# A conv and gated feed-forward kernel on one core: opening order of the first group, and the conv bias as a column

## The chip, the core and the metric

The kernel runs on one core of a Trainium2 chip. The metric is the device time of one launch in microseconds (us). A core has TensorE (PE in the profile; its weight loads are PEld), VectorE (DVE), ScalarE (ACT), GpSimd (POOL) and SyncE (SP), which here only issues DMAs. Each runs its own instructions in order and waits for the others through semaphores.

## What is computed

```python
# x 128x32x512, cond_128 128x128, fside_S_0 32
out = lax.conv_general_dilated(x, weight, window_strides=(1,), padding=[(4, 4)],
                               dimension_numbers=('NCH', 'OIH', 'NCH'), feature_group_count=4)
ctx = jnp.einsum('nd,od->no', c, c_weight)
out = out + ctx[:, :, None] + bias[None, :, None]
...
up = xt @ W_up.T            # xt: 4096 rows of 512; F = 1376
gate = jax.nn.silu(xt @ W_gate.T)
y = gate * up @ W_down.T
x = x + y
```

## The kernel before, in words

The 32 channels form four groups (`G`) of eight. For each group the conv output (1024 rows of 512) is the moving operand of the gate and up products, whose 1376 rows are taken in eleven chunks `f` of 128; then come the down products. Every fp32 product is made of three products of "hi" and "lo" parts (`terms`), so each weight and each operand is first split: ScalarE writes the hi part (line 843, `split_h`, `w_raw`, `w_mixed`), VectorE the lo part (line 1070).

From chunk 1 on, a chunk's gate and up blocks for both halves of the rows come from seven products (kinds 0 to 6) instead of eight, in the manner of Strassen and Winograd. These need sums of operands (`K_S1`, `K_S2`, `K_S3`, `K_S4`, made from the staged conv output by `mix_h_first`) and sums of weights (T1 and T2 by VectorE, lines 1134 and 1138; T3 and T4 by GpSimd, `mix_t`, lines 513 and 514, which then also makes their lo parts, line 521). `prepare(f, part)` is ScalarE's and VectorE's share of chunk f's weights: part 0 keeps the turned gate block, part 1 the up block and T1, T2; part 2 splits T1 and T2, part 3 splits T3 and T4. `RAW_A1`, `RAW_A2`, `RAW_B1`, `RAW_B2` are plain parts of the conv output; `q` counts their two K blocks. Chunk 0 of group 0 uses eight plain products (`first_half`, `second_half`, line 725), so that it can start before any sum exists.

Before that, TensorE turns the conv weights, the context weights (`turn_ctx`) and x, runs eight conv steps (lines 624 and 629), and makes `ctxb`, the context product plus bias, 128 rows per group, with two fp32 products per group: one with `cond_t` (line 576), one of a single contraction row, the repeated bias against a row of ones (line 577). VectorE adds `ctxb` as it reads each conv step out of PSUM (`read_conv`), SP re-lays each read step by DMA into `stage` (32 window DMAs, `stage_window`, line 336, two of them from ScalarE's queue), and behind these SP issues the loads of chunk 2's gate and up weights into `w_nat` (`load_nat(2)`) and of the next group's x (`load_x(1, 0)`). `wrap` is a copy of four columns that GpSimd makes for each loaded weight block; TensorE turns the block only after it. `block_x` is GpSimd's reordering of x for the next group's conv.

Every engine's order is written out by hand. Waits that matter below, in the kernel's words: `product(0, 1, 5)` (kind 5 of chunk 1, line 711) waits for `copied4`, which is ScalarE's `copy_chain(1, 1, 4)`, since it overwrites the bank that is copied; `product(0, 1, 1)` waits for `silu_a_done`, VectorE's first step of `first_gated(0)`, which follows ScalarE's `first_sigmoids`; `product(0, 1, 2)` waits for `w_made[K_S2]`, the lo part of T2; second_half's products wait per q for VectorE's lo part of `RAW_A2` and `RAW_B2`, whose source is the staged conv output.

## Time and profile before

| | us |
|---|---|
| median of three runs (764.04 to 764.9) | 764.38 |
| the profiled execution's own time | 765.41 |
| its span, first to last instruction | 763.6 |
| TensorE busy in the span | 749.9 |

The span is measured by the hardware profiler in one execution. What lies around it, 765.41 - 763.6 = 1.8 us, is launch and end. A timeline row reads: start and duration in us, engine, line, operation, output<-inputs, shapes and how many instructions are merged; in brackets how long the engine stood idle before it and what released it. Times are from the span's start.

### The profile page before, as it was taken

The page shows a single profiled execution, that of the slowest core. Times are in us where ns is not written, and L with a number is a line of the kernel's source. Part 1 is how long each engine was busy: PE and PEld are TensorE (multiplying, and loading weights), DVE is VectorE, ACT ScalarE, POOL GpSimd, SP SyncE. Part 2 cuts the span into 40 slices and gives each one's busy share as a digit, 9 for nine tenths or more (in the row PEclk, how much of TensorE's full clock was granted, in tenths as well). Part 3 has the DMA queues.
Part 4 walks back from the last instruction along what each step waited for, and adds up shares of the span by engine and source line. Part 5 has one row for each costly group of instructions (what it writes and reads, how often), then busy time and mean ns, then how long its engine had stood idle before and what let it go on. Part 6 is the DMA issues. An engine that isn't in the chain of part 4 may idle for free.

```text
span 763.6 us, 10287 instructions
## 1 busy us (share of the span) xinstructions
PE 749.9 (98%) x3465; PEld 611.4 (80%) x3465; DVE 426.9 (56%) x703; ACT 275.3 (36%) x519; POOL 79.6 (10%) x111
## 2 busy tenths in 40 slices
PE   7989999999999999999999999999999999999998
PEld 6768888878888887887888878787788888887886
DVE  3897776764765555446735545445763444445224
ACT  4555555443433233324422332233431233333221
POOL 4334434110000111001000100100000000000000
PEclk9999999999999999999999999999999999999999
DMA  6486666679988578667435867667443876766412
GB/s 184 125 316 235 222 226 236 219 221 312 356 266 262 166 206 221 172 179 218 163 114 187 268 176 209 193 191 218 140 140 109 295 197 195 193 191 181 140 27 111
DMA packets 113684, 152.37 MB, mean 200 GB/s; under 512 B 11138, under 2 KB 49186, under 8 KB 113634
## 3 DMA queue, kind: packets, MB, share of 16 engines
q1 hardware_dynamic: 113152, 151.51, 63.7%
q8 instruction: 29, 0.48, 0.3%
q10 hardware_dynamic: 482, 0.21, 0.1%
q14 instruction: 21, 0.17, 0.1%
HBM read 108.95 MB, written 34.34 MB: 188 GB/s over the span
## 4 chain that ended last, share of the span: by engine, by line
PE 90%; issue 3%; SPq 2%; DMA 2%; DVE 1%; POOL 1%; ACT 0%; POOLq 0%; DVEq 0%
PE bank L711 51%; PE bank L774 31%; PE bank L624 2%; PE bank L629 2%; PE bank L604 2%; SPq L336 2%; DMA stage<-win 1%; PE bank L667 1%; PE bank L638 1%; PE bank L649 0%; DVE g_all L1277 0%; POOL g_all L526 0%; PE bank L586 0%; DVE win L1162 0%; POOL t_all L513 0%
## 5 line engine op out<-in xcount | busy, mean ns | idle before, releaser
L711 PE MATMUL bank<-hc_hi,ring 128*128 128x512 f32 (+1 forms) x1204 | 376.5, 394 | 5.0 <-DVE ring L1070 2.0
L711 PEld LDWEIGHTS bank<-hc_hi,ring 128*128 128x128 f32 (+1 forms) x1204 | 219.5, 185 | 54.6 <-issue 5.0
L711 PE MATMUL bank<-hc_lo,ring 128*128 128x512 f32 (+1 forms) x602 | 235.1, 391 | 0.0
L774 PE MATMUL bank<-ring,g_hi 128*128 128x512 f32 (+1 forms) x704 | 218.6, 392 | 0.0
L774 PEld LDWEIGHTS bank<-ring,g_hi 128*128 128x128 f32 (+1 forms) x704 | 131.2, 188 | 28.0 <-DVE g_lo L1070 0.8
L843 ACT ACTIVATE mix<-bank 128x512 f32<-128x512 f32 (+1 forms) x129 | 77.1, 598 | 208.5 <-PE bank L711 208.5
L774 PE MATMUL bank<-ring,g_lo 128*128 128x512 f32 (+1 forms) x352 | 137.1, 390 | 0.0
L711 PEld LDWEIGHTS bank<-hc_lo,ring 128*128 128x128 f32 (+1 forms) x602 | 111.5, 185 | 26.2
L1070 DVE TENSOR_TENSOR g_lo<-g_all,g_hi 128x512 fp32r<-128x512 f32 (+1 forms) x88 | 60.9, 695 | 83.7 <-ACT g_hi L843 83.7
L843 ACT ACTIVATE g_hi<-g_all 128x512 fp32r<-128x512 f32 (+1 forms) x88 | 55.1, 629 | 114.1 <-PE bank L774 114.0
L1243 DVE TENSOR_TENSOR mix<-bank,mix 128x512 f32<-128x512 f32 (+1 forms) x43 | 29.7, 691 | 87.2 <-ACT mix L960 87.0
L774 PEld LDWEIGHTS bank<-ring,g_lo 128*128 128x128 f32 (+1 forms) x352 | 66.1, 188 | 14.1
L305 POOL COPY x_blk<-x_in 128x512 f32<-128x512 f32 x24 | 28.0, 1166 | 325.5 <-DMA x_in<-in_x 166.4
L1238 DVE TENSOR_TENSOR mix<-bank,mix 128x512 f32<-128x512 f32 (+1 forms) x43 | 29.5, 687 | 37.5 <-ACT mix L843 37.5
L1233 DVE TENSOR_TENSOR mix<-mix 128x512 f32<-128x512 f32 (+1 forms) x43 | 29.7, 692 | 34.8 <-ACT mix L954 34.7
L960 ACT ACTIVATE mix<-bank 128x512 f32<-128x512 f32 (+1 forms) x43 | 25.7, 598 | 43.2 <-PE bank L711 43.2
L1228 DVE TENSOR_TENSOR mix<-bank,mix 128x512 f32<-128x512 f32 (+1 forms) x43 | 29.7, 691 | 11.2 <-PE bank L711 6.0
L843 ACT ACTIVATE xt_hi<-bank 128x512 fp32r<-128x512 f32 (+1 forms) x33 | 15.9, 510 | 55.1 <-PE bank L604 55.1
L1248 DVE TENSOR_TENSOR mix<-bank,mix 128x512 f32<-128x512 f32 (+1 forms) x43 | 29.7, 691 | 8.1 <-PE bank L711 6.8
L1162 DVE TENSOR_TENSOR win<-bank,ctxb 128x512 f32<-128x512 f32 (+1 forms) x24 | 16.1, 670 | 30.4 <-DMA stage<-win 21.5
L1070 DVE TENSOR_TENSOR hc_lo<-stage,hc_hi 128x512 fp32r<-128x512 f32 x50 | 32.6, 691 | 0.8 <-ACT hc_hi L843 0.7
L843 ACT ACTIVATE hc_hi<-stage 128x512 fp32r<-128x512 f32 x50 | 28.6, 618 | 2.9 <-DMA stage<-g_all 2.8
(141 smaller groups left out, 562.1 us busy)
## 6 DMA issues: line engine op xcount, KB each, us to landing
ring<-saved SPq DMA_DIRECT2D x319, 256.0 KB, 2.9
saved<-ring SPq DMA_DIRECT2D x99, 256.0 KB, 2.6
g_all<-in_x SPq DMA_DIRECT2D x32, 256.0 KB, 3.7
out_y<-g_all SPq DMA_DIRECT2D x32, 256.0 KB, 3.6
x_in<-in_x SPq DMA_DIRECT2D x13, 512.0 KB, 5.1
stage<-win SPq DMA_DIRECT2D x96, 64.0 KB, 2.8
w_nat<-in_L_ffn_W_gate SPq DMA_DIRECT2D x10, 256.0 KB, 3.9
w_nat<-in_L_ffn_W_up SPq DMA_DIRECT2D x10, 256.0 KB, 3.9
```

The lines of the kernel that those rows point to most:

```text
L305: copy(blocks(grp, k)[:, :, :, :], x_place(grp, k // 2)[:, :, r0:r0 + WB * R] .rearrange("n c (b r) -> n b r c", r=R)).then_inc(x_blocked_ ...
L711: mm = pe.matmul(bank[0:w, :], wt, hv, start=fresh and q == 0 and t == 0, stop=q == 1 and t == 2, skip_group_check=not fresh)
L774: mm = pe.matmul(acc(half, tt)[:], gs, wd, start=f == 0 and t == 0, stop=f == FC - 1 and t == 2)
L843: return act.activation(dst, src, ACT.Copy)
L960: act.activation(act_b[0:w], chain_ps[f % 2][0:w, :], ACT.Sigmoid).then_inc(sig_b_done, 1)
L1070: return dve.tensor_tensor(dst, src, hi_part.bitcast(F32), ALU.subtract)
L1162: last = dve.tensor_tensor(to[:, w0:w0 + n, :], conv_bank(grp, k)[:, 0:n * P].rearrange("p (w n) -> p w n", w=n), ctxb[:, grp:grp + 1, :]. ...
L1228: dve.tensor_tensor(act_a[0:w], second_ps[0:w, :], copy0[0:w], ALU.add).then_inc(gate_a_done, 1)
L1233: dve.tensor_tensor(act_a[0:w], act_a[0:w], sig_a[0:w], ALU.mult).then_inc(silu_a_done, 1)
L1238: dve.tensor_tensor(copy4[0:w], third_ps[0:w, :], copy4[0:w], ALU.add).then_inc(up_b_done, 1)
L1243: dve.tensor_tensor(act_b[0:w], chain_ps[f % 2][0:w, :], act_b[0:w], ALU.mult).then_inc(silu_b_done, 1)
L1248: dve.tensor_tensor(copy2[0:w], third_ps[0:w, :], copy2[0:w], ALU.add).then_inc(up_a_done, 1)
```

## The change

Nothing is computed differently except the bias. Its parts:

1. The bias no longer enters by 1x128 products against a row of ones. `turn_ctx` makes four fp32 products of one output column each (the repeated bias of a group against one element of `ones`) into four spare columns of `gate_ps`; ScalarE copies these to `bias_col`, and `keep_ctx` now makes one activation per group with the column as its bias.
2. TensorE turns the up block of chunk 1 before `first_half` instead of behind it, and the context products of groups 1 to 3 stand between the q halves of `first_half`'s first product. The wait for the last conv read moves behind that product.
3. ScalarE and VectorE do all of chunk 1's `prepare` parts ahead of, or between, the splits of `RAW_A2` and `RAW_B2`; `K_S3`'s splits move behind those of `K_S1` and `K_S2`. GpSimd wraps chunk 2's weights first and does `mix_t(1)`, `mix_t_lo(1)` before `block_x(1, 0)`.
4. In chunk 1, `K_S4`'s splits move behind `prepare(2, 1)` and `prepare(2, 2)` on both engines; on ScalarE they now stand directly ahead of `copy_chain(1, 1, 4)`.

```diff
@@ gpsimd
             mix_h_first(1)
+            wrap(2)
             for g in range(G):
                 for f in range(FC):
-                    if g + 1 < G and f == 0:
-                        block_x(g + 1, 0)
-                    if g == 0 and f + 2 < FC:
+                    if g == 0 and 0 < f < FC - 2:
                         wrap(f + 2)
                     if g == 0 and f + 1 < FC:
                         mix_t(f + 1)
                         mix_t_lo(f + 1)
+                    if g + 1 < G and f == 0:
+                        block_x(g + 1, 0)
@@ tensor
-                pe.transpose(gate_ps[:, 0:P], cond_nat, ident[:]).then_inc(ctx_mm, 1)
+                pe.transpose(gate_ps[:, 0:P], cond_nat, ident[:])
+                pe.wait_ge(consts, 8)
+                for g in range(G):
+                    mm = pe.matmul(gate_ps[:, P + g:P + g + 1], bias_rep[:, g, :], ones[:, 0:1], start=True, stop=True, skip_group_check=True)
+                mm.then_inc(ctx_mm, 1)
...
                 for g in groups:
-                    to = ctx_bank(g)[:, g * P:(g + 1) * P]
-                    pe.matmul(to, ctx_w_rep[:, g, :, :], cond_t, start=True, stop=False)
-                    mm = pe.matmul(to, bias_rep[:, g, :], ones, start=False, stop=True)
+                    mm = pe.matmul(ctx_bank(g)[:, g * P:(g + 1) * P], ctx_w_rep[:, g, :, :], cond_t, start=True, stop=True)
...
             def first_half():
                 pe.wait_ge(t_lo_done, 1)
+                pe.wait_ge(w_made[RAW_A1], 1)
+                plain(RAW_A1, RAW_A1, second_ps, True, parts=(0,))
+                ctx_products(range(1, G))
+                plain(RAW_A1, RAW_A1, second_ps, True, parts=(1,))
                 pe.wait_ge(conv_out, CPG)
-                pe.wait_ge(w_made[RAW_A1], 1)
-                plain(RAW_A1, RAW_A1, second_ps, True)
...
             turn_gate(1)
-            ctx_products(range(1, G))
+            turn_up(1)
             first_half()
-            turn_up(1)
             second_half()
@@ scalar
             def keep_ctx(n, groups):
                 act.wait_ge(ctx_mm, n + 1)
-                hi(ctxb[:, groups, :], ctx_bank(n - 1)[:].rearrange("p (g n) -> p g n", g=G)[:, groups, :]).then_inc(ctx_done, 1)
+                for g in groups:
+                    last = act.activation(ctxb[:, g, :], ctx_bank(g)[:, g * P:(g + 1) * P], ACT.Identity, bias=bias_col[:, g:g + 1])
+                last.then_inc(ctx_done, 1)
...
             prepare(1, 0)
-            keep_ctx(2, slice(1, G))
-            split_h(0, K_S3, 0)
-            split_h(0, K_S3, 1)
-            for q in range(2):
-                split_h(0, RAW_A2, q)
-                split_h(0, RAW_B2, q)
             prepare(1, 1)
-            for kind in (K_S1, K_S2):
+            keep_ctx(2, range(1, G))
+            split_h(0, RAW_A2, 0)
+            split_h(0, RAW_B2, 0)
+            prepare(1, 2)
+            split_h(0, RAW_A2, 1)
+            split_h(0, RAW_B2, 1)
+            prepare(1, 3)
+            for kind in (K_S1, K_S2, K_S3):
                 split_h(0, kind, 0)
                 split_h(0, kind, 1)
             first_sigmoids()
-            prepare(1, 2)
-            prepare(1, 3)
...
                     sigmoid_a(n, f)
-                    if n == 1:
-                        split_h(0, K_S4, 0)
-                        split_h(0, K_S4, 1)
...
                         prepare(f + 1, 2)
+                    if n == 1:
+                        split_h(0, K_S4, 0)
+                        split_h(0, K_S4, 1)
                     copy_chain(n, f, 4)
@@ vector
             prepare(1, 0)
-            split_h(0, K_S3, 0)
-            split_h(0, K_S3, 1)
-            for q in range(2):
-                split_h(0, RAW_A2, q)
-                split_h(0, RAW_B2, q)
+            prepare(1, 1)
+            split_h(0, RAW_A2, 0)
+            split_h(0, RAW_B2, 0)
+            prepare(1, 2)
+            split_h(0, RAW_A2, 1)
+            split_h(0, RAW_B2, 1)
             for kind in (K_S1, K_S2):
                 mix_h_first(kind, 0)
                 mix_h_first(kind, 1)
-            prepare(1, 1)
+            split_h(0, K_S2, 0)
+            split_h(0, K_S2, 1)
             first_gated(0)
-            for kind in (K_S2, K_S1):
-                split_h(0, kind, 0)
-                split_h(0, kind, 1)
+            split_h(0, K_S1, 0)
+            split_h(0, K_S1, 1)
+            split_h(0, K_S3, 0)
+            split_h(0, K_S3, 1)
             first_gated(1)
-            prepare(1, 2)
...
-                    if n == 1:
-                        split_h(0, K_S4, 0)
-                        split_h(0, K_S4, 1)
...
                         prepare(f + 1, 2)
+                    if n == 1:
+                        split_h(0, K_S4, 0)
+                        split_h(0, K_S4, 1)
```

On VectorE, from the splits of the staged conv output (`hc_lo<-stage`) to the first gated result (`g_all<-bank,mix`), before; `g_all<-stage` and `g_all<-g_all,stage` are the sums of operands, `ring<-bank` and the two `t_all` rows are chunk 1's up block, T1 and T2:

```order
L1070 TENSOR_TENSOR ring<-x_gate,ring 128x256 x2
L1070 TENSOR_TENSOR hc_lo<-g_all,hc_hi 128x512 x2
L1070 TENSOR_TENSOR hc_lo<-stage,hc_hi 128x512 x4
L1177 TENSOR_TENSOR g_all<-stage 128x512 x2
L1181 TENSOR_TENSOR g_all<-g_all,stage 128x512 x2
L1070 TENSOR_TENSOR ring<-bank,ring 128x256
L1134 TENSOR_TENSOR t_all<-bank,x_gate 128x256
L1138 TENSOR_TENSOR t_all<-bank,t_all 128x256
L1218 TENSOR_TENSOR mix<-bank,mix 128x512
L1221 TENSOR_TENSOR g_all<-bank,mix 128x512
```

and in the changed program:

```order
L1075 TENSOR_TENSOR ring<-x_gate,ring 128x256 x2
L1075 TENSOR_TENSOR ring<-bank,ring 128x256
L1139 TENSOR_TENSOR t_all<-bank,x_gate 128x256
L1143 TENSOR_TENSOR t_all<-bank,t_all 128x256
L1075 TENSOR_TENSOR hc_lo<-stage,hc_hi 128x512 x2
L1075 TENSOR_TENSOR ring<-t_all,ring 128x256 x2
L1075 TENSOR_TENSOR hc_lo<-stage,hc_hi 128x512 x2
L1182 TENSOR_TENSOR g_all<-stage 128x512 x2
L1186 TENSOR_TENSOR g_all<-g_all,stage 128x512 x2
L1075 TENSOR_TENSOR hc_lo<-g_all,hc_hi 128x512 x2
L1223 TENSOR_TENSOR mix<-bank,mix 128x512
```

T1, T2 and their lo parts went ahead of the sums; the split of K_S3 left its place ahead of the staged parts and one pair of operand splits (K_S2) now stands ahead of the gated result.

On ScalarE, chunk 1 from the copy of its second chain bank (the first row) to the copy of its fourth (`mix<-bank`, the last but one row), before; `mix<-mix` is a sigmoid, `hc_hi<-g_all` the split of K_S4, `ring<-bank` and `ring<-t_all` are chunk 2's up block and T1, T2:

```order
L843 ACTIVATE mix<-bank 128x512
L954 ACTIVATE mix<-mix 128x512
L843 ACTIVATE hc_hi<-g_all 128x512 x2
L843 ACTIVATE ring<-bank 128x256
L843 ACTIVATE ring<-t_all 128x256 x2
L843 ACTIVATE mix<-bank 128x512
L843 ACTIVATE ring<-t_all 128x256 x2
```

and in the changed program:

```order
L847 ACTIVATE mix<-bank 128x512
L958 ACTIVATE mix<-mix 128x512
L847 ACTIVATE ring<-bank 128x256
L847 ACTIVATE ring<-t_all 128x256 x2
L847 ACTIVATE hc_hi<-g_all 128x512 x2
L847 ACTIVATE mix<-bank 128x512
L847 ACTIVATE ring<-t_all 128x256 x2
```

The two splits of K_S4 now stand between T1, T2 and the copy.

On ScalarE a little earlier, from the first splits of the staged A2, B2 parts to the sigmoids (L937, L939), in the changed program; before, the four `ring<-t_all` rows of chunk 1 all stood behind the two sigmoids, and K_S3's two splits ahead of the staged parts:

```order
L847 ACTIVATE hc_hi<-stage 128x512 x2
L847 ACTIVATE ring<-t_all 128x256 x2
L847 ACTIVATE hc_hi<-stage 128x512 x2
L847 ACTIVATE ring<-t_all 128x256 x2
L847 ACTIVATE hc_hi<-g_all 128x512 x6
L937 ACTIVATE mix<-bank 128x512
```

The second `ring<-t_all x2` splits T3 and T4, which GpSimd makes, and six operand splits and the sigmoids are queued behind it.

## Rows read from the trace of the kernel before

**Rows 1.** The page: busy time of each engine, share, instructions.

```profile
PE 749.9 (98%) x3465; PEld 611.4 (80%) x3465; DVE 426.9 (56%) x703; ACT 275.3 (36%) x519; POOL 79.6 (10%) x111
```

**Rows 2.** Waits of TensorE after 90 us: total, times, longest.

```profile
PE bank L711 <- DVE mix L1238: 1.9, 3, 0.8
```

**Rows 3.** Timeline of TensorE, 29 to 58 us.

```profile
29.38 0.39 PE L576 MATMUL bank<-g_all 128*128 128x128 f32 x2
...
31.78 0.72 PE L725 MATMUL bank<-hc_hi,ring 128*128 128x512 f32 x2
...
45.07 0.66 PE L638 MATMUL bank<-ident,w_nat 128*128 128x128 f32 x4 [0.27 <-POOL w_nat L505]
...
49.95 0.73 PE L711 MATMUL bank<-hc_hi,ring 128*128 128x512 f32 x2 [1.97 <-DVE ring L1070]
...
55.75 0.40 PE L711 MATMUL bank<-hc_lo,ring 128*128 128x512 f32 x1
57.35 0.70 PE L711 MATMUL bank<-hc_hi,ring 128*128 128x512 f32 x2 [1.20 <-issue]
```

**Rows 4.** Timeline of ScalarE, 36 to 58 us.

```profile
36.98 1.15 ACT L843 ACTIVATE hc_hi<-stage 128x512 fp32r<-128x512 f32 x2 [1.04 <-DMA stage<-g_all]
...
41.92 0.58 ACT L933 ACTIVATE mix<-bank 128x512 f32<-128x512 f32 x1
...
52.65 1.14 ACT L843 ACTIVATE hc_hi<-g_all 128x512 fp32r<-128x512 f32 x2
...
55.89 0.87 ACT L843 ACTIVATE ring<-t_all 128x256 fp32r<-128x256 f32 x2 [1.82 <-DVE t_all L1134]
56.67 0.58 ACT L843 ACTIVATE mix<-bank 128x512 f32<-128x512 f32 x1
```

**Rows 5.** Timeline of VectorE, 38 to 56 us.

```profile
38.86 1.29 DVE L1177 TENSOR_TENSOR g_all<-stage 128x512 f32<-128x512 f32 x2
...
42.54 0.69 DVE L1218 TENSOR_TENSOR mix<-bank,mix 128x512 f32<-128x512 f32 x1
...
43.87 3.44 DVE L1070 TENSOR_TENSOR hc_lo<-g_all,hc_hi 128x512 fp32r<-128x512 f32 x4
47.24 0.68 DVE L1218 TENSOR_TENSOR mix<-bank,mix 128x512 f32<-128x512 f32 x1
...
49.81 0.68 DVE L1228 TENSOR_TENSOR mix<-bank,mix 128x512 f32<-128x512 f32 x1
...
55.36 0.41 DVE L1134 TENSOR_TENSOR t_all<-bank,x_gate 128x256 f32<-128x256 f32 x1
```

**Rows 6.** The chain that ended last, 6 to 16 us: start, us, what.

```profile
6.78 1.93 PE bank L604 x8
...
9.52 0.72 PE bank L577 x2
...
13.23 1.28 PE bank L629 x3
...
15.20 0.70 PE bank L624 x3
```

**Rows 7.** Timeline of TensorE's weight loads, 9.4 to 10.1 us.

```profile
9.45 0.50 PEld L577 LDWEIGHTS bank<-g_all 1*128 1x128 f32 x2 [0.23 <-issue]
```

**Rows 8.** Timeline of SP's queue, 15 to 36 us.

```profile
15.27 19.66 SPq L336 DMA_DIRECT2D stage<-g_all  x30
34.97 0.59 SPq L352 DMA_DIRECT2D w_nat<-in_L_ffn_W_gate  x1
```

**Rows 9.** Tile w_nat, loads issued 34.5 to 36.1 us.

```profile
DMA to landing us min/median/max: 2.9/3.0/3.0
```

**Rows 10.** Timeline of GpSimd, 43 to 47 us.

```profile
43.29 1.12 POOL L305 COPY x_blk<-x_in 128x512 f32<-128x512 f32 x1 [14.29 <-DMA x_in<-in_x]
44.35 1.26 POOL L505 COPY w_nat<-w_nat 128x4 f32<-128x4 f32 x2
45.57 1.19 POOL L513 TENSOR_TENSOR t_all<-t_all,x_gate 128x256 f32<-128x256 f32 x1
```

More of the change, by code:

```diff
@@ L156, in adaln_ffn @@
         ones = res[0:1, 2, 256:256 + P]
+        bias_col = res[:, 2, 448:448 + G]
         bias_row = res[0:1, 2, 384:384 + G * CG]
@@ L570, in ctx_products @@
                 pe.wait_ge(cond_ready, 1)
-                pe.wait_ge(consts, 8)
                 if groups[0] > 0:
@@ L713, in product, with plain @@
                 mm.then_inc(product_done[kind], 1)
-            def plain(operand, weights, bank, start, done=None):
+            def plain(operand, weights, bank, start, done=None, parts=range(2)):
                 w = width(0)
-                for q in range(2):
+                for q in parts:
                     pe.wait_ge(hc_done[operand], q + 1)
@@ L990, in _ @@
             act.wait_ge(ctx_mm, 1)
+            hi(bias_col, gate_ps[:, P:P + G])
             hi(cond_t, gate_ps[:, 0:P]).then_inc(cond_ready, 1)
             split_x(0, 1)
-            keep_ctx(1, slice(0, 1))
+            keep_ctx(1, (0,))
             for k in range(STEPS):
@@ L1047, in _ @@
                         prepare(f + 1, 1)
-                    if more:
                         prepare(f + 1, 2)
+                    if n == 1:
+                        split_h(0, K_S4, 0)
+                        split_h(0, K_S4, 1)
                     copy_chain(n, f, 4)
@@ L1298, in _ @@
             prepare(1, 0)
-            split_h(0, K_S3, 0)
-            split_h(0, K_S3, 1)
-            for q in range(2):
-                split_h(0, RAW_A2, q)
-                split_h(0, RAW_B2, q)
+            prepare(1, 1)
[4 more added lines that the diff above has]
+            split_h(0, RAW_B2, 1)
             for kind in (K_S1, K_S2):
```

## The prediction

> **What bounds the kernel now.** The page comes first: TensorE is busy 749.9 of 763.6 us [rows 1], so only work that leaves TensorE or a wait that it stands in can change the time. The table of waits after 90 us shows 1.9 us in three small waits [rows 2], all in groups that the change does not touch; whatever shift the opening leaves is therefore carried to the end. The question is when TensorE starts kind 5 of chunk 1, the product behind the last wait of the opening. Before, that is 57.35 us [rows 3].
>
> Before it the timeline has three waits: 0.27 us for chunk 2's wrap, 1.97 us for the lo part of T2, and 1.20 us put down to "issue" [rows 3]. The kernel says what this last one is: kind 5 waits for `copied4`, and ScalarE's copy runs from 56.67 to 57.25 us [rows 4], 0.1 us ahead of TensorE's start. The copy stood behind the splits of chunk 2's T1 and T2, which began at 55.89 us after 1.82 us of idling for VectorE's T1 [rows 4], made from 55.36 to 55.77 us [rows 5]. VectorE in turn has no idle bracket from 42.54 us to there [rows 5]. So the opening ends by VectorE's work and then three ScalarE operations, and not by TensorE's. Shortening any wait ahead of it is worth nothing by itself. I follow this chain.
>
> **Term 1, the bias.** Removed: in the opening, one 1x128 product per group. At 9.52 us it took 0.72 us [rows 6]; the three later pairs took 31.78 - 29.38 = 2.40 us for six products, 0.40 us each [rows 3], so 1.2 us more. Added: four products of one column ahead of the turning of x. No row shows an fp32 product of one column. Each still loads its weights twice, and the two loads of the 1x128 product took 0.50 us [rows 7]; that is the nearest row, and I take 0.46 us, four times 1.85 us. From below: a transpose with as many weight columns and 128 moving ones took 1.93 / 8 = 0.24 us [rows 6], which bounds four at 0.96 us; from above the whole 0.72 us, 2.9 us. The net delay of the conv is 1.85 - 0.72 = +1.13 us, bounds +0.24 and +2.2 us.
>
> All this is at half rate: three conv products took 1.28 us at 13.23 us and 0.70 us at 15.20 us [rows 6], so TensorE stepped from 1.2 to 2.4 GHz at about 14.8 us, although the page's granted clock reads full throughout. If the step stays at that time, the work pushed behind it runs at the doubled rate and the delay shrinks to 1.13 x 0.70 / 1.28 = 0.6 us (bounds 0.1 and 1.2 us). I take 0.6 us. ScalarE's tiny copy of four columns and the bias operands of its three activations stand in its idle time.
>
> The Trainium skill, "TensorE: Matmul & The Clock Gate", sections "Back-to-back issue gap" and "LDWEIGHTS", has products of up to 64 columns at about 25 ns and a load at its columns over 1.2 GHz, 107 ns. By it the eight loads would take an estimated 0.85 us and the bias edit would cost almost nothing at 7 us. The 0.50 us of two loads here speaks for the dearer value.
>
> **Term 2, where TensorE's 1.2 us go.** Without the later bias products TensorE reaches `second_half` earlier. Its q = 1 needs the last staged windows. SP issued 30 of them from 15.27 to 34.93 us without pause worth naming [rows 8], and ScalarE's split of the last part waited 1.04 us for the landing, until 36.98 us [rows 4]. SP's queue starts with the first conv read, so it comes 0.6 us later, not earlier. ScalarE then splits A2 and B2 at 37.6 us, VectorE from 38.25 to 39.45 us. TensorE waits about a microsecond there, and the gain of 1.2 us is worth nothing.
>
> **Term 3, GpSimd ahead of ScalarE.** T3 and T4 of chunk 1 now need `wrap(2)` done, which needs load_nat(2): issued 34.97 us [rows 8], landing 2.9 to 3.0 us later [rows 9]; with 0.6 us of shift the up block, issued 0.63 us behind the gate block, lands at 39.2 us. The wrap ends at 39.5. A T sum took 1.19 us beside a busy VectorE [rows 10], so T3 is there at 40.65 and T4 at 41.8 us. ScalarE stands in order: it splits T4 until 42.15, and only then the six operand splits of K_S1, K_S2, K_S3 at 1.04 / 2 = 0.52 us each (52.65 to 53.69 us) [rows 4], until 45.25; the sigmoid, 0.6 us, ends at 45.85 us. Before, it ended at 42.5 [rows 4]. VectorE meanwhile makes the four sums from 39.45 us: 0.60 us each alone (38.86 us row), 0.86 us each beside GpSimd (3.44 / 4) [rows 5]; that is 42.9 us at the latest, then K_S2's lo parts, ready before 45.85. So VectorE too waits for the sigmoid.
>
> **Term 4, VectorE to chunk 2's T1.** From 45.87 us: the first gated pair 1.33 us (42.54 to 43.87), four lo parts 2.40 us (K_S1, K_S3, GpSimd idle by then), the second gated pair 1.32 us (47.24 to 48.56) [rows 5]: 50.9 us. Before, `prepare(1, 2)` came next and `gate_a` stood at 49.81 us; from there to T1's end, 55.77 us, are 5.96 us [rows 5], of which K_S4's lo parts (1.20 us) have moved behind: 4.76 us. T1 is done at 50.9 + 4.76 = 55.66 us, against 55.77. All that left VectorE's chain (T1, T2, two pairs of lo parts) is spent on waiting for ScalarE and on K_S3's lo parts, which used to fill a pause before the last landing.
>
> **Term 5, ScalarE to the copy.** T1's and T2's splits: 0.12 us behind T1, 0.78 us long (55.89 to 56.67 us), until 56.56. Then, new here, K_S4's two splits, 1.04 us, which stood in a pause of 1.82 us before [rows 4]: 57.6 us. The copy takes 0.58 us, TensorE starts 0.1 us later: 58.3 us, against 57.35. The sum is +0.95 us, and I call it +1.0 us. TensorE, with 15.3 us of work from the staged part on, would be there at about 54.6 us and would now stand some 3.5 us in this one wait. Behind it, kind 6 needs K_S4's lo parts and `up_b`, which VectorE ends by 59.4 us, while TensorE comes at 60.1: no further wait.
>
> The sum on its own execution is 765.41 + 1.0 = 766.4 us; this execution lay 1.03 us over the median of the runs shown, so beside the median it is 764.38 + 1.0 = **765.4 us**. A measurement of this kernel tells about 0.2%, 1.5 us, from no change. The terms' own bounds: term 1 moves the result from -0.5 to +0.6 us (everything behind it hangs on SP's start); the contention of sums and the GpSimd rows -0.3 to +0.4. The likeliest case's own range is 764.7 to 766.2 us.
>
> **Rivals.** (a) *It is faster, because ScalarE is not held.* If T3 and T4 were there before the last staged part, the sigmoid would follow the sums at once and VectorE would run from 39.45 us through: sums 2.4, K_S2 1.2, gated 1.33, lo parts 2.4, gated 1.32, then 4.76: 52.9 us for T1, 55.4 us for the copy, TensorE at 55.5, which is -1.85 us: 762.5 us. The point from which it decides is the landing of chunk 2's weights, which would have to come some 4 us earlier. The loads stand behind the same 30 windows as before [rows 8], so this speaks against it; only the unmerged cost of GpSimd's small copies could shift parts of it. Chance 0.10.
>
> (b) *The opening's slack takes it all.* If one-column products cost nearly what a load costs and VectorE's sums run free of GpSimd, terms 1 and 3 shrink by about 0.5 us each, and K_S4's splits on ScalarE are paid for by the earlier T1: no change, 764.4 us. For it speaks that T1 needs to come only a microsecond earlier. Against it: ScalarE's six splits behind T4, not the sums, set the sigmoid. Chance 0.20.
>
> (c) *The clock steps up later.* Before, the wide conv products began at 11.6 us and the step came at about 14.8. Now they begin a microsecond later and more narrow products stand before them. If the step follows them instead of the time, term 1 is the full 1.13 us, total +1.5 us; if the step is missed once and comes two or three microseconds later, each of these costs half its length again: total +2.5 us, 766.9 us. It decides if the first three wide products at half rate become many. The same page of the Trainium skill ("What's actually happening") says that the point of the step varies from run to run; then both kernels' medians would hold some of it. No second execution of before is shown that would tell. Chance 0.20.
>
> The forecast has the remaining 0.50.
>
> **How the numbers follow.** Slower by over 0.2% is above 765.9 us: all of (c), and the upper fifth of the likeliest case: 0.30. Faster is (a): 0.10. The rest is 0.60. The range goes from 764.1 us (the lower end of (b)) to 767.2 us ((c)); it leaves out (a) and the tails, about 0.2.
>
> **What would show it.** In the profile after: four one-column products at 6.8 us, 1.85 us in all; the first window DMA later than 15.27 us; a wait in `second_half` of about 1 us; GpSimd's first T sum at about 39.5 us; a wait of some 0.5 to 1 us before kind 1 of chunk 1, for the sigmoid; no wait of 1.97 us before kind 2; and one wait of 3 us or more before kind 5, ended by ScalarE's copy at about 58.2 us, directly behind K_S4's splits. The prediction is wrong if that start lies before 57 us, which needs the sigmoid well ahead of 44 us, or if half-rate products go on beyond 15 us.

## The result and the profile after

The changed kernel takes 767.29 us in the median of 20 runs (764.50 to 769.52), the kernel before 764.21 us in 20 runs beside it: ratio 1.0038, 95% interval 1.0027 to 1.0049. It is slower, by 3.1 us, three times the 1.0 us of the forecast, and 0.1 us above the top of the range. The profiled execution took 765.94 us, with a span of 764.1 us; only two of the 20 took less.

First the page's busy line after (it answers to [rows 1]) and the table of TensorE's waits after 90 us ([rows 2]):

```profile
PE 748.7 (98%) x3465; PEld 612.2 (80%) x3465; DVE 427.6 (56%) x703; ACT 275.6 (36%) x522; POOL 80.8 (11%) x111
```

```profile
PE bank L714 <- DVE mix L1243: 0.5, 1, 0.5
```

TensorE is as busy as before, and behind 90 us it has one wait of 0.5 us against 1.9 us in three before. The opening has to be read again. TensorE's timeline after, the four one-column products and the rows of the opening that have a wait in brackets ([rows 3]):

```profile
6.61 1.86 PE L571 MATMUL bank<-g_all 1*128 1x1 f32 x8
...
38.61 0.73 PE L728 MATMUL bank<-hc_hi,ring 128*128 128x512 f32 x2 [1.76 <-DVE hc_lo L1075]
...
46.99 0.70 PE L714 MATMUL bank<-hc_hi,ring 128*128 128x512 f32 x2 [1.52 <-issue]
...
58.63 1.19 PE L714 MATMUL bank<-hc_hi,ring 128*128 128x512 f32 x2 [3.21 <-issue]
59.62 0.63 PE L714 MATMUL bank<-hc_lo,ring 128*128 128x512 f32 x1
60.04 1.05 PE L714 MATMUL bank<-hc_hi,ring 128*128 128x512 f32 x2
60.90 0.63 PE L714 MATMUL bank<-hc_lo,ring 128*128 128x512 f32 x1
61.32 0.70 PE L652 MATMUL bank<-ident,w_nat 128*128 128x128 f32 x4
```

The waits stand where the prediction put them: one in `second_half`, one before kind 1, none before kind 2, and 3.21 us before kind 5, which starts at 58.63 us in place of 57.35. But the row of kind 5 itself reads 1.19 us for two products that took 0.70 us before. The granted clock says why. TensorE's windows, after and then before (us, busy time of each engine, PEclk, DMA share, GB/s):

```profile
55.00:58.60 3.60, 0.42 (x2) 0.00 (x1) 3.43 (x7) 2.43 (x6) 1.81 (x2) 0.93 0.39 146
58.60:62.00 3.40, 3.37 (x11) 2.71 (x12) 1.60 (x3) 1.46 (x4) 3.09 (x5) 0.57 0.48 181
62.00:66.00 4.00, 4.00 (x23) 3.43 (x22) 3.12 (x5) 1.77 (x5) 0.17 (x2) 1.00 0.84 278
```

```profile
58.60:62.00 3.40, 3.40 (x19) 2.82 (x18) 1.88 (x3) 2.35 (x6) 2.34 (x5) 1.00 0.63 229
```

While it stands idle TensorE falls from its level of 2.4 GHz to 1.2 GHz, and kind 5 runs at half rate: from its first product to the turning of the up block behind it are 61.32 - 58.63 = 2.69 us, against 58.79 - 57.35 = 1.44 us before (the row of the turning before is below). That is 1.25 us on top of the later start. The Trainium skill, "TensorE: Matmul & The Clock Gate", section "What's actually happening", states that the slow level is the default and that an idle stretch brings it back; the trace agrees, with 0.57 of the clock behind the wait of 3.21 us.

The turning behind kind 5 before, and then, much later, the last row of such a turning, before and after:

```profile
58.79 0.60 PE L649 MATMUL bank<-ident,w_nat 128*128 128x128 f32 x4
...
195.61 0.60 PE L667 MATMUL bank<-ident,w_nat 128*96 128x128 f32 x4
```

```profile
198.26 0.64 PE L670 MATMUL bank<-ident,w_nat 128*96 128x128 f32 x4
```

So the opening costs 198.26 - 195.61 = 2.65 us: 1.28 by the later start of kind 5, 1.25 by the clock, 0.1 in small pieces. That the spans differ by only 0.5 us is luck of this execution. Fewer waits stand behind the opening: counted from start to start of the products around them, the three waits of before pushed the rest back by 0.85, 0.99 and 0.51 us, the one after by 0.59, which is 1.8 us less. Some 0.35 us more are in no row that I can name.

The median of +3.1 us holds more than this execution's opening. A profile in which the clock fell once behind the first step reads a mean granted clock of 0.997 or 0.998 (this one 0.998, e0, e2, e5 and e6), with two falls 0.995 (e11), with three 0.993 (e3). Of the 20 runs 14 read 0.994 to 0.996, with a median of 767.5 us, and six 0.998 or 0.999, with one of 766.2 us. The profiled execution is one of the six.

ScalarE after ([rows 4]), VectorE ([rows 5]), GpSimd ([rows 10]) and SP's queue ([rows 8]):

```profile
41.00 0.42 ACT L847 ACTIVATE ring<-t_all 128x256 fp32r<-128x256 f32 x1 [2.65 <-POOL t_all L514]
...
42.47 3.22 ACT L847 ACTIVATE hc_hi<-g_all 128x512 fp32r<-128x512 f32 x6
45.59 0.57 ACT L937 ACTIVATE mix<-bank 128x512 f32<-128x512 f32 x1
...
56.13 0.87 ACT L847 ACTIVATE ring<-t_all 128x256 fp32r<-128x256 f32 x2 [3.25 <-DVE t_all L1139]
56.91 1.13 ACT L847 ACTIVATE hc_hi<-g_all 128x512 fp32r<-128x512 f32 x2
57.95 0.58 ACT L847 ACTIVATE mix<-bank 128x512 f32<-128x512 f32 x1
```

```profile
47.53 2.49 DVE L1075 TENSOR_TENSOR hc_lo<-g_all,hc_hi 128x512 fp32r<-128x512 f32 x4
...
55.61 0.41 DVE L1139 TENSOR_TENSOR t_all<-bank,x_gate 128x256 f32<-128x256 f32 x1
```

```profile
39.19 0.63 POOL L506 COPY w_nat<-w_nat 128x4 f32<-128x4 f32 x1 [0.56 <-DMA w_nat<-in_L_ffn_W_up]
39.77 1.19 POOL L514 TENSOR_TENSOR t_all<-t_all,x_gate 128x256 f32<-128x256 f32 x1
```

```profile
15.42 19.96 SPq L337 DMA_DIRECT2D stage<-g_all  x30
35.43 0.59 SPq L353 DMA_DIRECT2D w_nat<-in_L_ffn_W_gate  x1
```

The reader sees terms 3 to 5 row by row: GpSimd's T3 at 39.77 us, ScalarE held for it 2.65 us, six splits, the sigmoid at 45.59; T1 of chunk 2 at 55.61; and `K_S4`'s two splits (56.91) between T1, T2 and the copy (57.95), on which kind 5 waits.

### The profile page after: what moved, and what is told of

The parts are those of the page before. It is cut to its first block, busy times and chain, and to the rows that moved or that the text cites. A ratio compares the mean times of both kernels' runs of the same rounds, so it can differ in the third digit from the quotient of the medians.

```text
span 764.1 us, 10288 instructions
## 1 busy us (share of the span) xinstructions
PE 748.7 (98%) x3465; PEld 612.2 (80%) x3465; DVE 427.6 (56%) x703; ACT 275.6 (36%) x522; POOL 80.8 (11%) x111
## 4 chain that ended last, share of the span: by engine, by line
PE 94%; DVE 2%; SPq 2%; issue 1%; DMA 1%; ACT 0%; DVEq 0%
PE bank L714 53%; PE bank L779 31%; PE bank L627 2%; PE bank L632 2%; PE bank L607 2%; SPq L337 1%; PE bank L728 1%; PE bank L670 1%; PE bank L641 1%; PE bank L652 1%; DVE hc_lo L1075 0%; DVE g_all L1282 0%; DMA stage<-win 0%; DMA stage<-g_all 0%; PE bank L589 0%
```

## The experiments

Twelve runs, one of them (e0) the changed kernel again, each timed beside the kernel before. "Start" is kind 5's first product in the profiled execution, counted from the product behind TensorE's first wait in the conv (22.86 us before, 22.77 us after; the conv's mark), since the conv itself goes at a different pace in each execution. "Opening" is the last row of up turnings (195.61 us before, 198.26 us after) counted from the same mark. "Clock" is the mean over the granted clocks of all timed runs; that of before is from the 35 runs beside e0, and 0.9990 and 0.9995 beside the others.

| kernel | median, before beside it, us | ratio, 95% interval | start | opening | clock |
|---|---|---|---|---|---|
| before | 764.21 | | 34.49 | 172.75 | 0.9991 |
| changed, first | 767.29, 764.21 | 1.0038 (1.0027 to 1.0049) | 35.86 | 175.49 | 0.9961 |
| changed, again (e0) | 768.75, 765.12 | 1.0034 (1.0023 to 1.0046) | 36.57 | 176.25 | 0.9972 |
| e1, 12 products fill the wait | 767.18, 764.44 | 1.0038 (1.0025 to 1.0051) | 36.27 | 175.00 | 0.9988 |
| e13, 14 products fill it | 766.72, 764.36 | 1.0025 (1.0012 to 1.0037) | 36.32 | 175.07 | 0.9988 |
| e2, K_S4's splits back | 767.61, 764.44 | 1.0040 (1.0027 to 1.0054) | 35.34 | 176.06 | 0.9977 |
| e3, T3, T4 split late | 768.36, 764.44 | 1.0053 (1.0032 to 1.0074) | 37.54 | 177.43 | 0.9964 |
| e6, order without bias | 768.07, 764.44 | 1.0051 (1.0035 to 1.0068) | 36.15 | 176.07 | 0.9970 |
| e5, bias without order | 765.38, 765.12 | 0.9997 (0.9986 to 1.0008) | 35.16 | 173.35 | 0.9991 |
| e8, K_S4 moved alone | 764.90, 765.12 | 0.9997 (0.9985 to 1.0009) | 34.51 | 173.23 | 0.9985 |
| e9, order of its own | 764.97, 765.12 | 0.9990 (0.9978 to 1.0002) | 32.66 | 172.42 | 0.9997 |
| e11, changed, copy early | 766.42, 764.36 | 1.0025 (1.0013 to 1.0037) | 33.1 | 176.05 | 0.9973 |
| e12, before, copy early | 763.62, 764.36 | 0.9982 (0.9969 to 0.9996) | 33.49 | 171.93 | 0.9993 |
| e10, e9 and copy early | 762.27, 764.36 | 0.9968 (0.9954 to 0.9982) | 31.77 | 171.11 | 0.9996 |

The opening of one profiled execution goes with the medians within 1.3 us: +2.7 and +3.5 us for the changed kernel (+3.1 and +3.6 in the times), +2.3 for e1 and e13 (+2.7 and +2.4), +3.3 for e2 and for e6 (+3.2, +3.6), -0.8 for e12 (-0.7), -1.6 for e10 (-2.1). The widest apart are e11 (+3.3 against +2.1), whose profiled execution is the slowest of its twelve, and e3 and e8.

**e0, the changed kernel again.**

> The changed kernel once more, on the chip of the three below: +2.9 us against before by the result (ratio 1.0027 to 1.0049), a wait of about 3.2 us before kind 5 of chunk 1 and TensorE at its lower level behind it. If the fall of the clock is not in each execution, this profile may lack it.

Borne out, the fall too. Its profile shows 3.24 us of wait, 1.19 us for kind 5's first pair, and a start 0.7 us later against the conv than the first profile; SP's queue, below, says why.

**e1 and e13, the wait filled.** Ahead of kind 5:

```diff
+                    if g == 0 and f == 1:
+                        filler(12)      # 14 in e13
                     product(g, f, 5)
...
+            def filler(count):
+                pe.wait_ge(g_done[1], 1)
+                for n in range(count):
+                    pe.matmul(conv_ps[:], up1_w(0, 0, P), hc_hi[:, RAW_A1, 0, :], start=True, stop=True)
```

> The changed kernel with twelve unused 128x512 products on TensorE directly ahead of kind 5 of chunk 1, where it otherwise stands idle for 3.21 us; they overwrite a conv bank that nothing reads any more, and the output is unchanged. Their own time is at most 12 x 0.23 = 2.8 us at full rate, so they fit into the wait. Theory (clock): the wait itself only costs what the late copy costs, and the fall of TensorE to its lower level behind it costs another 1.3 to 1.5 us (kind 5 and kind 6 at 1.19 us for two products that took 0.70 us before). Then kind 5 starts at the same 58.6 us, its first two products take 0.70 us, the granted clock stays at 1.00 from 58.6 to 62 us, and the median is 1.3 to 1.5 us under the changed kernel: about +1.3 us against before. Rival (the fall comes for another reason, or is recovered later): kind 5's first two products still take about 1.2 us and the time stays at about +2.9 us.

> The changed kernel with fourteen unused products in the wait before kind 5 in place of twelve, so that next to nothing of the wait is left; they are 14 x 0.23 = 3.2 us, as long as the wait. With twelve the trace showed no lower clock behind the wait, but the time was +2.7 us against before, where +1.3 to +1.5 us were expected. If the clock's part is real, the mean granted clock of these executions is 0.999 or more and the median is 0.7 to 1.5 us below that of the changed kernel: +1.4 to +2.3 us against before. If the clock's fall costs nothing that the median shows: +2.9 us or more.

TensorE's timeline of e1, the filler and kind 5:

```profile
56.11 2.89 PE L735 MATMUL bank<-hc_hi,up 128*128 128x512 f32 x12
59.49 0.70 PE L714 MATMUL bank<-hc_hi,ring 128*128 128x512 f32 x2 [0.49 <-issue]
```

The wait is full of work, and kind 5's pair takes 0.70 us again, at a start that lies among those of the changed kernel; from start to the turning are 1.46 us against 2.69. In e13's profile too nothing behind the wait is at half rate. So the idle stretch is what lowers the clock. The times do not repeat the 1.25 us cleanly: +2.7 and +2.4 us against before, where the changed kernel has +3.1 and +3.6 us. That is 0.3 to 1.3 us less, with intervals that overlap, and e1's ratio of 1.0038 is no lower than the changed kernel's; e13's bound of 2.3 us was missed by 0.1, its clock of 0.999 by a little. The traces show what the filling is worth: from kind 5's start to the last up turning are 138.73 us (e1) and 138.75 us (e13), 139.63 and 139.68 us in the changed kernel's two profiles, 138.26 us before. So 0.9 us come back and not 1.25, because a wait of 0.2 us stands before kind 6 that the half rate had covered. Eight of the 18 runs of e1 and e13 have a mean clock of 1.0, two of 32 of the changed kernel; that the others lose theirs behind the waits in `second_half` and before kind 1, which are not filled, is likely and not shown.

**e2 and e3, the two causes on ScalarE taken back one by one.** In the change `prepare(1, 3)` stands on ScalarE behind both pairs of splits of the staged parts.

```diff
@@ e2, scalar
                     sigmoid_a(n, f)
+                    if n == 1:
+                        split_h(0, K_S4, 0)
+                        split_h(0, K_S4, 1)
...
-                    if n == 1:
-                        split_h(0, K_S4, 0)
-                        split_h(0, K_S4, 1)
                     copy_chain(n, f, 4)
@@ e3, scalar
             split_h(0, RAW_B2, 1)
-            prepare(1, 3)
...
             first_sigmoids()
+            prepare(1, 3)
             copy_chain(1, 1, 0)
```

> The changed kernel with K_S4's two splits on ScalarE back behind the sigmoid, so that they lie in the pause before T1 of chunk 2. Term 5 of the prediction: the copy of the fourth chain bank comes 1.0 us earlier, kind 5 starts at 57.6 us in place of 58.6, behind a wait of about 2.2 us. If a wait of 2.2 us leaves TensorE at its upper level (waits of 1.97 us did in the kernel before), the clock's 1.4 us go too: about -2.4 us against the changed kernel, +0.5 us against before. If it still falls: -1.0 us against the changed kernel, +1.9 us against before. Rival (the copy is not what kind 5 waits for): the start stays at 58.6 us and the time at +2.9 us.

ScalarE in e2, and TensorE behind it:

```profile
56.92 0.88 ACT L847 ACTIVATE ring<-t_all 128x256 fp32r<-128x256 f32 x2 [1.38 <-DVE t_all L1139]
57.70 0.58 ACT L847 ACTIVATE mix<-bank 128x512 f32<-128x512 f32 x1
```

```profile
58.38 0.84 PE L714 MATMUL bank<-hc_hi,ring 128*128 128x512 f32 x2 [2.17 <-issue]
```

From the split of T1 to kind 5 are 58.38 - 56.92 = 1.46 us, in the changed kernel 58.63 - 56.13 = 2.50, before 57.35 - 55.89 = 1.46: term 5's 1.04 us to the hundredth, and the wait is 2.17 us. The same holds in every profile in which kind 5 stands for the copy: it starts 1.98 or 1.99 us behind T1's start on VectorE in before, e2 and e9, and 3.02 or 3.03 us in the seven with K_S4's splits ahead of the copy (changed twice, e1, e3, e6, e8, e13).

Yet the time does not fall. The clock fell at this wait as well (0.84 us for the first pair, 1.06 for the next), so the condition of the first theory, that 2.2 us are short enough, is not met. All of the half rate now lies on products, since none of it passed in the wait: it costs 1.7 us here against 1.25. T1 came 0.5 us later than in the first profile of the changed kernel, and small waits between 195 and 199 us, the last of 0.29 us for a load, take another 0.7. So in the traces the 1.04 us are gained before kind 5 and lost behind it (opening 176.06 against 175.49 and 176.25), as the times say.

> The changed kernel with ScalarE's splits of T3 and T4 of chunk 1 back behind the first sigmoids, nothing else. Term 3 of the prediction says that ScalarE, standing at T3 for GpSimd, makes VectorE's chain late by way of the sigmoid: then the sigmoid ends 2 to 3 us earlier than 46.2 us, T1 of chunk 2 comes earlier than 55.6 us, kind 5 starts ahead of 58.6 us by the same, and the wait is shorter. Rival: VectorE's chain is held elsewhere (by the sums beside GpSimd, or by a new wait for block_x, which stands behind mix_t_lo on GpSimd and there needs ScalarE's splits of T3 and T4): then the sigmoid is early, but T1 of chunk 2 stays at 55.3 to 55.8 us or later, TensorE meets a wait in the conv of the next group, and the time stays at +2.5 to +3.5 us against before.

The rival was right. VectorE and GpSimd in e3, behind the first gated pair:

```profile
47.24 4.04 DVE L1075 TENSOR_TENSOR hc_lo<-g_all,hc_hi 128x512 fp32r<-128x512 f32 x4
```

```profile
46.75 1.89 POOL L522 TENSOR_TENSOR ring<-t_all,ring 128x256 fp32r<-128x256 f32 x2 [3.61 <-ACT ring L847]
48.58 1.55 POOL L306 COPY x_blk<-x_in 128x512 f32<-128x512 f32 x1
```

Counted from the split of the last staged part (38.24 us in e3, 37.20 us in the changed kernel) the sigmoid comes 45.30 - 38.24 = 7.06 us later in place of 8.39: 1.3 us gained, as term 3 has it. But GpSimd's lo parts of T3 and T4 now wait for ScalarE, run from 46.75 us beside VectorE's four lo parts, and these take 4.04 us in place of 2.49. The gain is given back within 4 us, and T1 of chunk 2 comes 0.2 us later, not earlier (18.63 us behind the split in place of 18.41). The time, +3.9 us, is above even the rival's 3.5 us. To move these splits alone thus gains nothing. The profiled execution of e3 is its slowest, 772.07 us: the clock fell three times in it, behind waits of 2.55, 3.10 and, at 306.0 us, 2.07 us.

**e5 and e6, the bias and the order apart.** e5 is the kernel before with `turn_ctx`, `ctx_products` and `keep_ctx` of the change; e6 is the changed kernel with those three as before.

> The kernel before with the bias part of the change alone: four one-column products ahead of x, one activation per group, no product of one contraction row. The order of all else is that of before. Term 1: +0.6 us, the first window DMA at 15.9 us in place of 15.27 us and all behind it later by that. Rival: hidden, because the clock steps up at another time (0.0 us), or a gain, because 1.2 us of the later bias products go and TensorE's waits do not take them all (-0.5 us).

> The changed kernel with the bias as before (products of one contraction row, no column); all changes of order stay. Term 1 of the prediction gives the bias +0.6 us: then the first window DMA is issued 0.6 us earlier than in the changed kernel when both are read by medians, and the time is about +2.3 us against before. Rival (the bias part is hidden by the earlier step of the clock, as in the one profiled execution, or saved again by the three later products): the time is that of the changed kernel, +2.9 us, with the same wait of about 3 us before kind 5 and the same fall of the clock behind it.

The bias costs nothing that the times can tell (e5: 0.9997, an interval from -1.1 to +0.6 us), and without it the change is no better (e6: 1.0051, +3.6 us). In the eight profiles with the column the conv's first wait ends at 22.03 to 23.34 us, on average 22.83; in the six without it at 22.46 to 23.64, on average 23.12. The spread inside either set goes with the step of the clock in the conv, which comes earlier or later from one execution to the next. A wide conv product before, and one at the same time in the changed kernel:

```profile
13.88 0.63 PE L629 MATMUL bank<-hc_lo,tb_hi 128*128 128x512 f32 x1
```

```profile
13.80 0.39 PE L632 MATMUL bank<-hc_hi,tb_hi 128*128 128x512 f32 x1
```

In this pair the step came a microsecond earlier in the changed kernel; e6, without the column, still has 0.63 us at 14.00, e11, with it, 0.39 us at 13.06. The trace's first record of the granted clock, at its full level, gives the time of the step. In e8, without the column, and e13, with it, it is 13.88 us in both, and the conv's mark is

```profile
22.46 0.47 PE L629 MATMUL bank<-hc_hi,tb_hi 128*128 128x512 f32 x1 [0.59 <-DVE hc_lo L1069]
```

```profile
22.82 0.47 PE L632 MATMUL bank<-hc_hi,tb_hi 128*128 128x512 f32 x1 [0.57 <-DVE hc_lo L1082]
```

so 0.36 us later with the column; between before (step at 14.89 us, mark 22.86) and e1 and e0 (14.66 and 15.08 us, marks 23.22 and 23.34) it is some 0.4 us. Term 1's delay is thus there, at two thirds of its 0.6 us. But over all profiles the step came earlier with the column (12.1 to 15.1 us) than without it (13.9 to 16.6 us), and that hides it. Whether the column brings the step forward or this is chance, no run shows.

The 1.2 us that the later bias products gave back went into waits: e5 stands 2.99 us before kind 2 (1.97 before), and there too the clock fell:

```profile
50.56 0.73 PE L713 MATMUL bank<-hc_hi,ring 128*128 128x512 f32 x2 [2.99 <-DVE ring L1075]
...
52.09 1.06 PE L713 MATMUL bank<-hc_hi,ring 128*128 128x512 f32 x2
```

**e8, K_S4's splits moved in the kernel before, on both engines, as the change has it.**

> The kernel before with K_S4's splits of chunk 1 moved behind the splits of chunk 2's T1 and T2 on both engines, as in the change, and nothing else. VectorE gains 1.2 us ahead of T1 of chunk 2, ScalarE loses 1.0 us behind it: kind 5 starts between 57.0 and 57.4 us, the time is -0.2 to 0.0 us against before. Rival: moved splits alone are what costs (kind 5 at 58.3 us and a wait above 2 us): +1.0 us, or +2.4 us with the clock's fall.

As expected: kind 5 at 56.97 us, 34.51 us behind the conv's mark against 34.49, ratio 0.9997. T1 starts 31.49 us behind the mark in place of 32.50, and that 1.0 us pays for the 1.04 us of the splits. The move costs where VectorE does not pay for it with an earlier T1.

**e9, an order of its own.** The changed kernel without the bias column and with

```diff
@@ scalar (vector: the K_S3 splits alone)
             split_h(0, RAW_B2, 0)
+            split_h(0, K_S3, 0)
+            split_h(0, K_S3, 1)
             prepare(1, 2)
...
-            prepare(1, 3)
-            for kind in (K_S1, K_S2, K_S3):
+            for kind in (K_S1, K_S2):
...
             first_sigmoids()
+            prepare(1, 3)
```

and e2's edit.

> A version meant to beat both kernels: the changed kernel without the bias column, K_S3's splits back in the pause before the last staged parts on ScalarE and VectorE, T3's and T4's splits behind the first sigmoids on ScalarE, K_S4's splits back behind the sigmoid on ScalarE alone. If the two causes named are right (ScalarE held behind T3, K_S4 ahead of the copy), VectorE reaches T1 of chunk 2 about 2 us earlier than before and kind 5 starts at about 55.3 us with a wait under 1.5 us and no fall of the clock: -1.5 to -2.2 us against before. Rival: another wait takes their place (GpSimd's block_x, the wrap of chunk 2, or the staged windows) and the time is that of before.

Kind 5 starts at 55.63 us, 1.8 us earlier against the conv, and the clock stays up. But 1.21 us of wait before kind 6 (for `up_b`) and 0.78 us before the turning of x (for `block_x`) take that back: 0.9990, an interval that includes no change. The rival was right about the sum.

**e11, e12 and e10, the copy ahead of T1 and T2.** e2 and e9 show that kind 5 is tied to VectorE's T1 only through ScalarE's order: the copy reads a bank that kind 4 has long filled. The same two moves in the changed kernel (e11), the kernel before (e12) and e9 (e10):

```diff
@@ scalar
                     if more:
                         prepare(f + 1, 1)
+                    if n == 1:
+                        copy_chain(n, f, 4)
+                    if more:
                         prepare(f + 1, 2)
-                    copy_chain(n, f, 4)
+                    if n > 1:
+                        copy_chain(n, f, 4)
@@ vector
                         prepare(f + 1, 1)
+                    if n == 1:
+                        up_b(n, f)
+                    if more:
                         prepare(f + 1, 2)
```

e10 also splits K_S4 ahead of T1 on VectorE and puts `block_x(1, 0)` between `mix_t(1)` and `mix_t_lo(1)` on GpSimd.

> The changed kernel with two moves in chunk 1 only: ScalarE's copy of the fourth chain bank ahead of the splits of chunk 2's T1 and T2 (and so of K_S4's splits), VectorE's up_b ahead of T1's and T2's lo parts. If the copy's place behind these splits is the cause of the 3.2 us wait, the wait before kind 5 is gone (start at about 55.5 us), TensorE stands instead before kind 6 for K_S4's lo parts, 1.3 to 2.0 us, and the clock does not fall: -1.3 us from the wait and -1.4 us or more from the clock against the changed kernel, about +0.3 us against before. If the clock falls at the new wait too: about +1.7 us against before. Rival (kind 5 needs T1 or something else of VectorE's chain): kind 5 still starts at 58 us or later.

> The kernel before with the same two moves (copy of the fourth chain bank ahead of the splits of T1 and T2 on ScalarE, up_b ahead of their lo parts on VectorE). The prediction says that the opening of the kernel before ends by VectorE's T1, then three operations of ScalarE, the copy last, at 57.35 us. If only the copy's place in ScalarE's order ties kind 5 to T1, the 1.20 us wait goes, kind 5 starts at 56.1 us and the time is -1.1 us against before (ratio 0.9985). Rival: another wait of the same length stands behind it (up_b before kind 6): 0.0 us.

> The version before (bias products as before, K_S3's splits in the pause ahead of the last staged parts, T3's and T4's splits behind the first sigmoids) with its three remaining waits taken away: ScalarE's copy of the fourth chain bank in chunk 1 goes ahead of the splits of chunk 2's T1 and T2, VectorE's K_S4 lo parts ahead of and up_b directly behind the making of T1 and T2, and GpSimd's block_x between mix_t and mix_t_lo. If the waits before kinds 5 and 6 (0.27 and 1.21 us) and for x_blk (0.78 us) are what is left, TensorE reaches kind 5 at about 54.5 us and has no wait over 0.3 us between 40 and 66 us: -2.0 to -2.8 us against before (ratio 0.9963 to 0.9974). Rival: the contention of VectorE and GpSimd or later waits take it back: -0.5 us as measured for the version before.

TensorE's waits between 30 and 66 us (total, times, longest) in e12 and then in e10:

```profile
PE bank L711 <- DVE ring L1073: 1.9, 1, 1.9
PE bank L638 <- POOL w_nat L505: 0.6, 1, 0.6
```

```profile
PE bank L727 <- DVE hc_lo L1077: 0.8, 1, 0.8
PE bank L606 <- POOL x_blk L305: 0.5, 1, 0.5
```

The wait before kind 5 is gone in both. e12 is faster than the kernel before, ratio 0.9982 (0.9969 to 0.9996, so only just clear of no change), by two moves; -1.1 us was expected, the medians say -0.7, and kind 5 starts 1.0 us earlier against the mark. e10 is faster still: 762.27 us, 0.9968 (0.9954 to 0.9982), 2.1 us under before and the shortest of the set. Two waits over the 0.3 us that its expectation allowed are left, as the lines show.

In e11 kind 5 starts without a wait, and TensorE stands for K_S4's lo parts before kind 6, as expected, though for 2.59 us and not 1.3 to 2.0:

```profile
56.51 0.62 PE L652 MATMUL bank<-ident,w_nat 128*128 128x128 f32 x4
59.72 1.05 PE L714 MATMUL bank<-hc_hi,ring 128*128 128x512 f32 x2 [2.59 <-DVE hc_lo L1079]
```

The pair takes 1.05 us: the clock fell again, and +1.7 us was the expectation for that; measured +2.1 us. This profile also holds a fall of a second kind, in the plain products behind the wait for the last staged parts (1.93 us at 38.50 us). TensorE's window there:

```profile
39.00:43.00 4.00, 4.00 (x13) 3.09 (x12) 3.53 (x5) 1.41 (x4) 4.00 (x4) 0.57 1.04 359
```

e3's profile has the same behind 2.55 us of wait. That is where the slower of the changed kernel's runs, 14 of the first 20 with a clock that one fall does not give, may lose more than the profiled one; no profile of one of them is there to show it.

## Why the prediction was off by two thirds

Of the three outcomes the prediction gave most, 0.60, to a change of under 0.2%; the one that came, slower by more than that (0.38%), had 0.30. The path was right and the place: TensorE's opening ends in one wait before kind 5, ended by ScalarE's copy directly behind K_S4's splits. Point by point:

- **Term 1, the price of a one-column product: right.** 1.86 us against 1.85. **What it does to the end: not told by the times, 0.4 us by the traces at an equal step of the clock.** The step moves by more between executions than the edit moves the conv, and the likeliest case took it as fixed.
- **Term 2: right, and mis-sized.** The gain of 1.2 us went into the wait in `second_half`, 1.76 us in place of "about a microsecond", 2.42 us in e0. I had SP's queue later by the 0.6 us of term 1. It was later for another reason, below.
- **Term 3: right as a chain, wrong as a cause.** GpSimd's T3 at 39.77 (39.5 was given), the sigmoid starting at 45.59 and over by 46.16 (45.85). e3 shows that without it the time is no better.
- **Term 4: near.** T1 done at 56.02 us (55.61 + 0.41) in place of 55.66; up to 0.3 us of it by GpSimd's copy of four columns, 0.63 us where I had 0.3.
- **Term 5: the sum ended at the wrong point.** Kind 5 at 58.63 us in place of 58.3, and K_S4's part of it exact (e2). But the prediction took the wait of "some 3.5 us" as a time shift alone. It says that TensorE "would now stand some 3.5 us in this one wait", and goes on at full rate. The step that failed is this one: the half rate behind the wait was put at nothing, without a reason, and it costs 1.25 us in the profile (2.69 us for work that took 1.44). Rival (c) had the right mechanism, the clock, at the wrong place: it priced only a late first step at 13 to 15 us, and looked for the half rate nowhere else. That its 766.9 us lie near the measured time is luck.

The sum with what was measured, against the conv's mark: the start 1.4 to 2.1 us later, the clock 1.25 us, together 2.6 to 3.3 us; the medians say 3.1 and 3.6 us. Of the start's shift, 1.04 us are K_S4's splits, and the rest is T1 of chunk 2. By term 4 it was to come 0.1 us earlier than before; against the mark it came 0.34 us later (32.84 us in place of 32.50) and 1.05 us later in e0.

A row that the prediction had no term for goes with that. SP's queue around 32 to 34 us, before, after and in e0:

```profile
32.40 1.89 SPq L336 DMA_DIRECT2D stage<-g_all  x3
```

```profile
32.28 2.46 SPq L337 DMA_DIRECT2D stage<-g_all  x3
```

```profile
32.21 2.48 SPq L337 DMA_DIRECT2D stage<-g_all  x2
```

An issue of a window takes 0.60 us. In the changed kernel's two profiles one of them takes 1.16 and 1.83 us, and all that SP issues behind it, the last windows and chunk 2's weights, is later by the rest. This is so in each of the ten profiles with the new order ahead of the staged parts, on GpSimd (`wrap(2)` first) as on ScalarE, VectorE and TensorE (1.16 to 1.92 us, mean 1.6, at 31.8 to 34.5 us; e3 has another of 1.29 us at 15.7), e9 and e10 among them, and in none of the four with the old one (before, e5, e8, e12), where the first load of chunk 2's weights is issued 12.10 us behind the conv's mark each time, against 12.66 to 14.02 us. So the order costs the staged parts 0.6 to 1.9 us. It is 0.55 us in the first profile of the changed kernel and 1.22 us in e0, near T1's 0.34 and 1.05; that T1 is late by it is argued from this, and no run takes it away. What holds the issue is not shown by any run here. It stays open.

## What to carry to other kernels

A wait of TensorE of about 2 us or more can cost more than its length, so the sum of a prediction has to say at which clock the products behind it run. In an order written by hand, look for the operation that is ready but queued behind one that is not: here a copy whose input was long there stood behind two splits that waited for VectorE, and moving it, with the addition that needs it, made the kernel before faster. Work that is moved off one engine's path onto a time when its neighbour is busy can cost there what it gained (e3: four lo parts 4.04 us in place of 2.49).

## What the runs showed of the hardware

- TensorE's products went to twice their time behind waits of 3.21 and 3.24 us at once, behind 3.10 and 3.23 us (e3, e6) after the first pair, behind 2.99 us (e5) only 1.3 us into the work, and behind 2.59 and 2.17 us (e11, e2) as well. Behind 1.97 us (before), 2.17 us (e13), 2.25 us (e2) and 2.42 us (e0) they did not, behind 1.93 us (e11), 2.07 us and 2.55 us (e3) they did. So the length of the wait alone does not decide, and the same code can keep or lose the clock from one execution to the next.
- The column of the granted clock reads 1.00 in the first 13 us, where the products run at half rate all the same (0.63 us for one that takes 0.39 later). The traces hold no record of the clock before the step to the full level, which comes at 12.1 to 16.6 us in the 14 profiles, so the column says nothing there.
- One of 30 equal DMA issues on SP took 1.16 to 1.92 us in place of 0.60 in ten of 14 profiles, those with the new order of the other engines' work (e3 has two); the cause is open.
- GpSimd's copies of 128x4 elements for one chunk took 0.19 us (38.44 us) and 0.63 us (39.19 us) in the changed kernel's profile; the second is a term of the delay of T3.
